# Two recurrent gated layers on one core: who starts the transfer of the maximum row in layer 1

## The reference, cut to what matters

```
q = (query @ Wq.T) -> 32 half heads of 8;  k likewise;  v -> 16 heads of 16
attn = softmax(q @ k.T * scaling + causal)            # for 32 half heads, 512 x 512
attn = attn[:, :, 0] - lam * attn[:, :, 1]
out = attn @ v;  rms norm per head;  out @ Wo.T
```

## Time and the profile before

| what | value |
|---|---|
| median of 3 runs | 2289.54 us (2276.5 to 2292.45) |
| profiled execution, its own time | 2289.04 us |
| its span, first to last instruction | 2287.3 us |
| PE busy | 2018.3 us (88%) |
| DVE busy | 1411.2 us (62%) |
| ACT busy | 885.4 us (39%) |
| POOL busy | 665.0 us (29%) |
| `qring<-mneg`, x96, 8.0 KB | median 2.6 us from issue to landing |
| `kring<-k_img`, x64, 256.0 KB | median 3.1 us from issue to landing |

### The profile page before, as it was taken

One profiled execution on the slowest core, in us unless ns is written; L12 is line 12 of the kernel. 1 busy time (PEld: TensorE's weight loads), 2 busy tenths in 40 slices (PEclk: granted clock), 3 DMA queues, 4 the chain that ended last, 5 costly groups with the idle time before them and its releaser, 6 DMA issues.

```text
span 2287.3 us, 33198 instructions
## 1 busy us (share of the span) xinstructions
PE 2018.3 (88%) x11778; PEld 1447.6 (63%) x11874; DVE 1411.2 (62%) x3219; ACT 885.4 (39%) x1749; POOL 665.0 (29%) x831
## 2 busy tenths in 40 slices
PE   2389899998999889998999989998999999999888
PEld 1257567576666766676675766757666676667656
DVE  4565675756666666656757567575665667665664
ACT  2143352524524244333534335251452425433352
POOL 2332331413313233223323233141331323222331
PEclk8589999999999999999999999999999999999999
DMA  6812523244231532216331252324423253221630
GB/s 208 300 47 90 165 75 107 65 122 130 61 109 62 163 111 70 74 56 185 103 94 56 91 160 80 107 65 126 122 60 102 74 172 102 80 82 39 180 98 15
DMA packets 105604, 240.47 MB, mean 105 GB/s; under 512 B 17048, under 2 KB 27288, under 8 KB 105184
## 3 DMA queue, kind: packets, MB, share of 16 engines
q1 hardware_dynamic: 91184, 194.41, 28.5%
q0 software_dynamic: 14256, 43.94, 6.7%
HBM read 179.67 MB, written 57.82 MB: 104 GB/s over the span
## 4 chain that ended last, share of the span: by engine, by line
PE 62%; DMA 11%; SPq 7%; DVE 7%; issue 3%; ACT 3%; POOL 0%; ACTq 0%; DVEq 0%; POOLq 0%
PE bank L420 20%; PE bank L582 12%; PE bank L503 11%; PE bank L469 8%; DMA qring<-mneg 7%; PE bank L519 5%; SPq L378 5%; DMA upring<-up_img 3%; PE bank L601 2%; DVE nmax L760 2%; PE bank L476 2%; DMA k_img<-probs 1%; ACT probs L660 1%; SPq L361 1%; ACT shared L630 1%
## 5 line engine op out<-in xcount | busy, mean ns | idle before, releaser
L420 PE MATMUL bank<-xnT,upring 128*128 128x512 f32 (+1 forms) x2208 | 721.8, 413 | 27.8 <-DMA upring<-up_img 27.6
L660 ACT ACTIVATE probs<-bank 128x512 f32<-128x512 f32 (+1 forms) x752 | 407.2, 557 | 394.6 <-PE bank L503 370.8
L503 PE MATMUL bank<-qring,kring 128*128 128x512 f32 (+1 forms) x1056 | 439.1, 419 | 107.1 <-DMA qring<-mneg 65.3
L760 DVE TENSOR_REDUCE nmax<-bank 128x2 f32<-128x512 f32 (+3 forms) x544 | 354.1, 658 | 218.4 <-PE bank L476 204.2
L469 PE MATMUL bank<-kring,qring 127*128 127x512 f32 (+3 forms) x1536 | 449.4, 346 | 34.3 <-DMA kring<-k_img 24.3
L420 PEld LDWEIGHTS bank<-xnT,upring 128*128 128x128 f32 x2208 | 416.3, 198 | 88.9 <-issue 30.8
L757 DVE CUSTOM_DVE_ANT_0 bank<-bank,mask_strip 128x512 f32<-128x512 f32 (+1 forms) x512 | 320.1, 635 | 164.2 <-PE bank L469 162.8
L469 PEld LDWEIGHTS bank<-kring,qring 127*128 127x128 f32 x1536 | 276.6, 195 | 123.2 <-DMA kring<-k_img 26.6
L503 PEld LDWEIGHTS bank<-qring,kring 128*128 128x128 f32 x1056 | 205.6, 196 | 214.1 <-DMA kring<-k_img 74.4
L582 PE MATMUL bank<-wdown,hbuf 128*128 128x256 f32 x1408 | 327.5, 382 | 0.0
L582 PEld LDWEIGHTS bank<-wdown,hbuf 128*128 128x128 f32 x1408 | 260.2, 191 | 32.7 <-issue 1.7
(11 more groups left out here) (127 smaller groups left out, 1862.4 us busy)
## 6 DMA issues: line engine op xcount, KB each, us to landing
upring<-up_img SPq DMA_DIRECT2D x176, 512.0 KB, 4.7
q_img<-probs SPq DMA_DIRECT2D x96, 256.0 KB, 3.2
qring<-q_img SPq DMA_DIRECT2D x256, 64.0 KB, 2.1
kring<-k_img SPq DMA_DIRECT2D x64, 256.0 KB, 3.1
qring<-q_img SPq DMA_DIRECT2D x32, 384.0 KB, 4.7
k_img<-probs SPq DMA_DIRECT2D x48, 256.0 KB, 4.5
up_img<-hbuf POOLq DMA_DIRECT2D x22, 512.0 KB, 4.9
gring<-gate_img POOLq DMA_DIRECT2D x32, 256.0 KB, 3.8
```

Source lines behind the costliest of these rows:

```text
L420: last = nc.tensor.matmul(out_ap, part_a(a, pa, k), part_b(b, pb, k), start=(n == 0), stop=(n == len(steps) - 1))
L503: nc.tensor.matmul(SC[n % 2][:, 0:heads * w].rearrange("p (g n) -> p g n", g=heads), kring[l][:, ks, kt * P:(kt + 1) * P], qring[l][:, s, ...
L660: nc.scalar.activation(pr, pr if biased else scores, ACT.Exp, scale=scale).then_inc(s_exp, 1)
L760: nc.vector.tensor_reduce(nmax[:, u % 2, g0:g0 + heads, qt], MX[n % 2][:, 0:heads * w].rearrange("p (g n) -> p g n", g=heads), AX.X, ALU.m ...
```

## The change

The row of units 5 to 11 is no longer issued by SP at the end of `rest_of_unit`. ScalarE issues it, directly behind its own copy. The same `max_row` is called with the other engine, so the wait for the copy and the semaphore that TensorE waits for stay the same. The rows of units 0 to 4 stay with SP.

```diff
@@ SP, rest_of_unit(u)
                     if not last_of_layer(u) and not last_of_layer(u + 1):
                         sp.wait_ge(s_sc, so_far(s_sc, PACKS * (u + 1)))
                         ring_load(sp, u + 2)
-                    if not last_of_layer(u):
-                        max_row(sp, u + 1)
@@ ACT, unit(u)
                         if i == PACKS - 1 and third_apart(u):
                             act_max_copy(act, u + 1)
+                            max_row(act, u + 1)
                         if i == 1 and u not in U0:
                             act_pv_copy(act, u - 1)
```

## The result

The kernel became a little slower. Its median is 2293.9 us (2286.36 to 2302.72, 19 runs) against 2286.33 us (2272.7 to 2295.62, 19 runs) of the kernel before on the same chip; the ratio is 1.004 with a 95% interval of 1.0024 to 1.0056. That is 7.6 us more where 7 us less was forecast. Each ratio in this document is taken from fast executions alone; of all experiments only keys first with ScalarE's row had slow ones, two of its six (2868.04 and 9822.69 us).

A forecast was written before the change was run, and what follows sets the result against it. PE was taken to wait at 48 boundaries for the maximum row, landing just behind the ring. Lag gained 9.3 us less 2.4 us for sharing gives 7 us: 2289.5 - 7 = 2282 us, range 2267 to 2299.

The forecast's parts named there:

- the ring is a wall of its own: At unit boundaries, SP's query and key loads land 0.17 to 0.27 us before the row and bind PE next.
- ScalarE's issues: On ACT, 56 row issues at 0.51 us, 28.6 us in all, fit its 3.57 us wait for PE and cost nothing.
- Boundary 10: Last boundary, eight times, no ring load: moving the row costs nothing, at most 2.4 us if ACT's issue is slower.
- The row starts earlier on ACT.: Row issued 0.03 us behind the copy's end instead of 0.25 or more, landing 2.3 us later, no later than the ring.
- My bounds: Row's time from ACT's issue to landing: 1.8 us with nothing around, 2.7 us queued behind a ring; 2.3 taken.
- The first rival: At boundaries, the row still lands with the ring or 0.17 us behind it; no gain, 2289.5 us; chance 0.2.
- The sum: Over 48 boundaries, 9.3 us of lag gained less 2.4 us for sharing: net gain 7 us.
- The lag to be gained: Row's landing behind the ring: 0.17 us in six batches, 0.27 in two, six boundaries each; 9.3 us in all.
- the weight load that moves up: On SP, the 512 KB load follows the keys 0.55 us sooner; its cost is within 0.05 us charged per boundary.
- the 7.4 us landing: Keys at layer 1's front, weight load behind them, took 7.4 us in one batch; 3.1 us elsewhere was taken as nearer.
- The slower rival: At boundaries, ACT's issue and the weight load delay the keys by up to 0.51 us; 15 us slower, 2304; chance 0.16.

The follow-up runs named there:

- keys first with ScalarE's row: The kernel after the change, with the 256 KB of keys issued before the four query pieces in layer 1's ring loads; ratio 0.9926 to the kernel before.
- the split issue: Kernel after, keys issued before queries, weight load held until the row lands, plus ScalarE issuing two of four query pieces; 0.9826 to the kernel before (0.9865 without the last).
- the run held at the first boundary only: Kernel after the change, with SP's weight load held until the row lands only at each batch's boundary from unit 4 to 5; ratio 0.9962 to the kernel before.
- the run whose long boundary was cut to 2.7 us on average: Kernel after, keys issued first, weight load held, ScalarE issuing two of four query pieces, one gate load issued later; 2239.1 us, 0.9807 to the kernel before.

## Why the prediction was wrong

**Right.** PE waits for two things at nearly the same time, and the ring is a wall of its own, 0.17 us in front of the row's landing: at seven boundaries the row had landed first, and PE still waited for the ring. ScalarE's issues cost it nothing: ACT busy is unchanged (885.4 and 885.3 us) and its first exponential still waits for PE. Boundary 10 did not change by more than 0.5 us in all.

**The step that failed: "The row starts earlier on ACT."** I took 2.3 us from issue to landing, "since the ring is in flight but the row is no longer behind it in one queue". It took 3.0 us at the median of the 56, and landed 0.170 us behind the ring. My bounds were 1.8 and 2.7, and from them followed that the row comes no later than the ring over the whole range. Both bounds were rows with a common queue or with nothing in flight; neither was a row issued beside 512 KB of another queue. The first rival had the mechanism, with 0.2 of the chance, and the argument that I weighed against it (a common queue would give the same steady lag) was an argument for neither. The runs showed in its place: a small transfer lands behind the large ones that were issued before it and are still in flight, whichever engine issued it, and one more small one ahead of it added 0.165 us. The Trainium skill's "DMA: Bandwidth & Descriptors", section "Queues, rings and completion order", says that an increment lands only behind the earlier writes of its DMA engine, across queues. The 0.170 us in a separate queue agree with it, and so does the row that lands with a weight load when there is no ring. The page says nothing of the 0.16 us.

The sum had two smaller faults that cancel in part. The lag to be gained was 48 x 0.163 = 7.8 us and not 9.3, as the 0.27 us of two batches came from landings rounded to 0.1 us. And the lag was not all that an earlier row is worth: PE starts about 0.3 us behind the ring where the row decides and 0.04 us where the ring does, so each boundary would have given 0.26 us. At the seven boundaries where the row did come first it gave that, 1.8 us in all by this estimate.

**The term that was mis-sized: the weight load that moves up.** I charged 0.05 us at every boundary for it and the sharing. At five of six boundaries that was fair (138.2 to 137.4 us with the earlier rows). At the first boundary of the layer, where GpSimd's gate load is in flight as well, it was 0.37 us a batch, 3.0 us in all, and some clock behind the longer idle time. The row had been a spacer between the keys and 512 KB of weights. That the weight load's place matters at this boundary because of the gate load is argued from where the loss sits: no run moves the gate load with the weight load left right behind the keys. I had named the 7.4 us landing as a warning and set it aside. I also read the boundaries as alike, though the earlier trace rows give a longest landing of 4.6 and 4.4 us beside medians of 3.0 and 3.5. Both are the first boundary of their batch, the one with the gate load.

**The slower rival** had its place right (the ring slips) and its cause half wrong: not two issues that hinder each other, as the split issue shows, but the load behind. Its 2304 assumed the slip everywhere.

**What stays open.** About 1 us of the 7.6, and how much of the clock's 3.4 us is its own: a longer wait and a lower clock come together in these runs, and the split between them is an estimate. Nor do the parts add up for the run held at the first boundary only: it is 0.0078 below the kernel after, 18 us, of which the boundary gives 5.8 us and 0.0034 of clock, at 1.6 us for 0.001, about 5 us. And why a small transfer lands 0.16 us behind the one before it, no run here shows.

## What to carry to other kernels

Before you move a small urgent transfer to another engine's queue, look at what is in flight when it starts: it landed 1.8 us after its issue alone, and 0.16 to 0.17 us behind the 512 KB of the ring from either engine. What helped here was to hold back the transfer that nobody waits for (from 1.004 to 0.9956 with ScalarE's row; 0.9983, at the edge of the noise, with SP's), to put the slow piece of a group first (0.9909), and to keep the background load of another engine away from the longest wait (35.5 to 28.6 us at that boundary). When you take an instruction out of a queue, ask what it was keeping apart.

## What the runs showed of the hardware

- A row issued by ScalarE lands at the same 0.16 to 0.17 us behind SP's ring as one issued by SP behind it. With one more 8 KB transfer ahead of it the lag is 0.330 us.
- Without the ring the row lands 3 us or more from its issue at 38 of 40 boundaries where a 512 KB load was issued 0.62 us before it, and 1.8 us at 13 of 16 where none was.
- With the weight load held as well, the row lands 1.8 us from its issue at 34 boundaries, and later at 22: at 9 a gate load is in flight, at 13 an `instruction` packet of 8 or 16 KB; beside the packets of the 34 there is neither.
- The granted clock fell to its 1.2 GHz level behind some of the PE idle times of about 3 us and not behind others; it fell behind 1.80 us and stayed behind 3.40 us. In the run whose long boundary was cut to 2.7 us on average, no unit ran at the lower clock.
